# Attention scores on 32-row products of four row groups, in a perceiver kernel on one core

## The chip, the cores and the metric

The kernel runs on one core of one Trainium2 chip, as one program written engine by engine: TensorE (PE, with its weight loads PEld), VectorE (DVE), ScalarE (ACT), GpSimd (POOL) and SyncE (SP), which here only issues DMAs. The engines meet at semaphores. The time is that of the core on the device, in microseconds (us), as the median of several runs.

## What is computed

Two batches of 128 latent tokens of 256 features attend to 2048 context rows each, twice, with other blocks between:

```python
x = x + L0_xattn(norm(x), ctx)   # 16 heads of 128, softmax(q k) v, per batch
x = x + L0_attn(norm(x))         # rotary, cosine similarity, a linear mix
x = x + L0_ffn(norm(x))          # top 2 of 8 experts
x = x + L1_xattn(norm(x), ctx)   # below
x = x + L1_attn(norm(x))         # dilated attention in segments of 64
x = x + L1_ffn(norm(x))          # block floating point, silu(gate) * up
```

The change touches the fourth, whose 16 heads have 16 dimensions, and whose queries see the keys of both batches, 4096 in all:

```python
q = quant((x @ Wq + bq) * scale)            # per query and head, 127 levels a side
k = quant(ctx @ Wk + bk)                    # per key and head
v = quant(ctx @ Wv + bv)                    # per head and dimension, over all keys
a = softmax(q @ k.T)                        # 128 x 4096 for a head of a batch
a = round(a / (max(a) / 255)) * (max(a) / 255)
x = x + (a @ v) @ Wp + bp
```

## The kernel before, in words

**Stages.** Until about 440 us the first cross attention runs, as 32 units (a head of a batch each; `sp_cross`, `pool_cross` and their like for PE, ACT and DVE). On the side POOL quantises the second attention's keys, tile by tile of 128 keys (lines 764 to 782), SP turns each tile by a DMA transposition into `kT` (lines 640 to 644), and the mix, the experts and the queries of batch 0 follow. From about 442 to 660 us the quantised attention runs, again as 32 units of a head of a batch, 16 for each batch. The mix, experts and queries of batch 1 and the output, dilated attention and feed-forward of batch 0 are woven into it as side work, at numbered slots, four to a unit (`Side`, `woven`). A short tail follows.

**A unit of the quantised attention.** The scores of a head are eight products of 512 keys. They are computed twice. The *firsts* (`pe_first`) run 12 products ahead, only for the maxima: DVE reduces each (`dve_first`, line 1892), POOL folds eight maxima into a bias. The *seconds* (`pe_second`) run in pairs, and ACT takes the exponential of each pair, 1024 keys, with that bias (`act_exponentials`, line 1885). SP turns each half of the result, 2048 keys, by a DMA transposition (`sp_attention`, line 1980), and PE multiplies the turned half by the values, 16 products of 16 columns (`attend`, line 1908), two units after the unit itself. PE's order in each quarter of a unit is fixed: two seconds, two firsts, in the first two quarters one half of `attend`, then side work. PE waits for exponentials before seconds (`q_exp`), for maxima before firsts (`q_max`; three PSUM banks take turns), for landings before `attend` (`q_turned`). Each engine takes its program in order, so what stands behind a waiting instruction waits too. In SP's queue the transpositions share the order with loads for later stages (`sp_ahead`).

**Scores.** A key has 16 dimensions in a high and a low fp16 part, 32 rows of `kT` for a head. `kT` holds four heads on its 128 partitions, and a product contracts all 128 rows (`pe_scores`, line 1843) against a query tile in which the rows of the other three heads are zero. That tile, `qT`, is made for each batch by POOL, which clears it (`pool_queries`, line 1833), by DVE, which writes the quantised queries twice for high and low (line 1775), by PE, which transposes four tiles (`pe_queries`, line 1793), and by ACT, which copies 32 rows at a time into place, four times (`act_queries`, line 1812). Batch 0 does that at the end of the first cross attention, batch 1 at slots 55 to 60 of the quantised one. `pe_first` waits for ACT's copies of a batch before the first head that uses each; where a side program shares its PSUM bank with `attend`, PE may also have to wait until the copies are done (`pe_leave`).

Of the kernel before, what the change touches and what calls it, by code (L numbers as in the profile page):

```python
# [19 lines left out]
P = 128  # L20
# [37 lines left out]
QUARTERS = 4  # L58

# [26 lines left out]
    kv k_biased v_biased v_abs k_steps k_rounded k_cut k_turned0 k_turned1 mx_steps mx_round mx_done mx_turned  # L86
    v_scale_pe v_scale_dve v_rounded_dve v_rounded_pool
    mix_pe0 mix_act0 mix_dve0 mix_pool0 ex_pe0 ex_act0 ex_dve0 qu_pe0 qu_act0 qu_dve0
    mix_pe1 mix_act1 mix_dve1 mix_pool1 ex_pe1 ex_act1 ex_dve1 qu_pe1 qu_act1 qu_dve1
# [10 lines left out]
CONSTANTS = steps("zeros ones minus_half ident ident16 ident_fp16 iota iota_f q_zeros0 q_zeros1")  # L100
# [10 lines left out]
QU_PE = steps("xT q qT")  # L111
QU_ACT = steps("xT qT0 qT1 qT2 qT3")
# [28 lines left out]
QU_WOVEN = "norm xT q both qT+copies copies1 copies2+copies3"  # L141
# [4 lines left out]
QU_AT = dict(norm=(29, 1), apply=(29, 3), xT=(30, 1), q=(30, 3), both=(31, 0), qT=(31, 2), copies=(31, 3))  # L146
# [65 lines left out]
class Tiles:  # L212


    def __init__(self, nc, stack):
# [18 lines left out]
        self.qT = upper[:, 0:UNITS * P].rearrange("p (b a r c) -> p b a r c", b=B, r=KG, c=P)  # L234
        self.q_both = upper[:, UNITS * P:(UNITS + KG * B) * P].rearrange("p (b h t d) -> p b h t d", b=B, h=H1, t=2)
# [3 lines left out]
        self.kT = sb("kT", [P, H1 // KG, KT * P], FP16)  # L239
# [78 lines left out]
class ContextTiles:  # L318


    def __init__(self, nc, stack):
# [8 lines left out]
        self.k_tmp = sb("k_tmp", [P, D])  # L330
# [4 lines left out]
        self.k_full = sb("k_full", [P, D])  # L335
        self.k_parts = sb("k_parts", [P, 2, H1, 2, HD1], FP16)
# [274 lines left out]
def sp_cross(sp, m, c, d, g, s, t):  # L611
    for u in range(UNITS + 2):
        if u == 0:
            sp.wait_ge(s["qk_mm"], 2)
            sp_load_early(sp, c, d, s, t, 3)
        elif u == 1:
            sp.wait_ge(s["qk_mm"], 3)
            sp_load_pair(sp, c, s, t, FIRST_PAIR)
        elif u + 2 < SPLIT:
            sp.wait_ge(s["qk_mm"], u + 2)  # L620
            sp_load_early(sp, c, d, s, t, u + 2)
# [30 lines left out]
        if u == H0:  # L652
            sp.wait_ge(s["k_turned0"], 16 * H0)
            sp.wait_ge(s["k_turned1"], 16 * H0)
            sp_load_slice(sp, g, s, t, 0)
            sp_load_slice(sp, g, s, t, 1)
# [81 lines left out]
def pool_cross(pool, m, c, d, g, s, side):  # L738
    full = d.k_full.rearrange("p (h d) -> p h d", h=H1)
    for u in range(UNITS + 3):  # L740
# [26 lines left out]
        for kt in (2 * u, 2 * u + 1) if u < H0 else ():  # L767
            ints = d.k_int[:, kt % 2, :].rearrange("p (h d) -> p h d", h=H1)
            scale = spread(d.k_scale[:, kt % 2, :], 2, HD1)
            hi, lo = (d.k_parts[:, kt % 2, :, n, :] for n in range(2))  # L770
# [772 lines left out]
def pe_mix(pe, m, x, s, b, room, at):  # L1543
# [3 lines left out]
    if b > 0:  # L1547
        pe.wait_ge(s["added"], UNITS)
        pe.wait_ge(s[f"qu_act{b - 1}"], QU_ACT["qT3"])
# [194 lines left out]
def dve_queries(dve, m, s, b, room, at):  # L1744
# [29 lines left out]
    for part in range(2):  # L1774
        dve.tensor_scalar(m.q_both[:, b, :, part, :], heads, ROUND, -ROUND, ALU.add, ALU.add).then_inc(sem, 1)


def pe_queries(pe, m, s, b, room, at):
# [10 lines left out]
    yield at["qT"]  # L1789
    pe.wait_ge(s[f"qu_dve{b}"], QU_DVE["both1"])  # L1790
    q_all = flat(m.q_both[:, b])
    for g in range(H1 // KG):
        ins = pe.transpose(room[2].bitcast(FP16)[:, g * P:(g + 1) * P], q_all[:, g * P:(g + 1) * P],
                           m.ident_fp16[:, :])
    ins.then_inc(sem, 1)
    if room.shared:
        yield from pe_leave(pe, room, at["copies3"], s[f"qu_act{b}"], QU_ACT["qT3"])


def act_queries(act, m, s, b, room, at):  # L1800
# [4 lines left out]
    yield at["copies"]  # L1805
    act.wait_ge(s[f"qu_pe{b}"], QU_PE["qT"])
    act.wait_ge(s["constants"], CONSTANTS[f"q_zeros{b}"])
# [20 lines left out]
def pool_queries(pool, m, s, b, room, at):  # L1828
    yield at["norm"]
    pool_normed(pool, m, s, b, NORM["attend"], room, m.x_res[:, b, :], m.xn[:, b, :])  # L1830
    pool.wait_ge(s["v_rounded_dve"], KT // 4)
    pool.wait_ge(s["v_rounded_pool"], KT // 4)
    pool.memset(m.qT[:, b], 0.0).then_inc(s["constants"], 1)
# [28 lines left out]
def pe_second(pe, m, s, u, q):  # L1862
# [10 lines left out]
    for k in range(CHUNK // BLK):  # L1873
        ins = pe_scores(pe, m, u, m.bank(second_place(u, q) + k), q * CHUNK + k * BLK)
# [21 lines left out]
def pe_attention(pe, m, x, s, side):  # L1896
    def attend(z, half):
# [9 lines left out]
        for j in range(KT // NH):  # L1907
            ins = pe.matmul(m.bank(7)[:, h * HD1:(h + 1) * HD1], x.yT[:, z % 2, half * KT // NH + j, :],  # L1908
                            m.v_int[:, half * KT // NH + j, h * HD1:(h + 1) * HD1], start=half == 0 and j == 0,
                            stop=half == 1 and j == KT // NH - 1)  # L1910
# [61 lines left out]
def sp_attention(sp, m, x, a, s, t):  # L1972
    sp.wait_ge(s["pv"], UNITS)
    for u in range(UNITS - 1):
# [8 lines left out]
        sp_ahead(sp, a, s, t, u)  # L1983

# [39 lines left out]
def dve_output(dve, m, x, s, b, half, room, at):  # L2024
# [11 lines left out]
    if b == 0 and half == 0:  # L2036
# [602 lines left out]
```

## Time and profile before

| what | value |
|---|---|
| median of 3 runs | 688.6 us (687.6 to 690.27) |
| profiled execution, span | 687.7 us |
| time around that span, by the profile | none recorded |
| PE, PEld busy | 651.0 us (95%), 410.1 us (60%) |
| DVE, ACT, POOL busy | 576.4 us (84%), 417.5 us (61%), 389.1 us (57%) |
| chain of waits by engine | PE 67%, DVE 21%, ACT 5%, issue 3%, DMA 2% |
| line 1843, score products, 512 of them | 140.4 us busy, mean 389 ns |

The span is cut into engines' busy shares, and a chain of waits leads from the last instruction back to the start. PE's mean of one instruction includes the overlap with the next: PE is pipelined, and on the chain four score products take 0.86 us. An engine that idles off the chain costs nothing. A whole-span share is an average over stages, so the stretches of the quantised attention are read one by one.

### The profile page before, as it was taken

The page shows a single profiled execution, that of the slowest core. Times are in us where ns is not written, and L with a number is a line of the kernel's source. Part 1 is how long each engine was busy: PE and PEld are TensorE (multiplying, and loading weights), DVE is VectorE, ACT ScalarE, POOL GpSimd, SP SyncE. Part 2 cuts the span into 40 slices and gives each one's busy share as a digit, 9 for nine tenths or more (in the row PEclk, how much of TensorE's full clock was granted, in tenths as well). Part 3 has the DMA queues.
Part 4 walks back from the last instruction along what each step waited for, and adds up shares of the span by engine and source line. Part 5 has one row for each costly group of instructions (what it writes and reads, how often), then busy time and mean ns, then how long its engine had stood idle before and what let it go on. Part 6 is the DMA issues. An engine that isn't in the chain of part 4 may idle for free.

```text
span 687.7 us, 13890 instructions
## 1 busy us (share of the span) xinstructions
PE 651.0 (95%) x5088; PEld 410.1 (60%) x5088; DVE 576.4 (84%) x1029; ACT 417.5 (61%) x697; POOL 389.1 (57%) x500
## 2 busy tenths in 40 slices
PE   8899999999999999999999999999889889988887
PEld 6456766666666676766766666654436444544453
DVE  5998987887897797899989769888877889999655
ACT  5644454444544465565654445549878899899941
POOL 5876666566557736689965516526635543345401
PEclk9999999999999999999999999999989999999999
DMA  9666689765756588988974965639998899999900
GB/s 309 164 147 140 146 184 172 173 140 122 158 122 151 120 196 215 210 173 193 184 168 118 226 144 115 148 81 218 235 186 153 168 149 198 160 185 163 201 14 9
DMA packets 347827, 111.01 MB, mean 161 GB/s; under 512 B 313704, under 2 KB 344432, under 8 KB 347760
## 3 DMA queue, kind: packets, MB, share of 16 engines
q1 hardware_dynamic: 347760, 110.13, 77.1%
q8 instruction: 41, 0.67, 0.4%
q14 instruction: 26, 0.21, 0.1%
HBM read 31.97 MB, written 0.26 MB: 47 GB/s over the span
## 4 chain that ended last, share of the span: by engine, by line
PE 67%; DVE 21%; ACT 5%; issue 3%; DMA 2%; POOL 1%; DVEq 0%; ACTq 0%; POOLq 0%
PE psum L1060 21%; PE psum L1032 20%; DVE tops L1892 8%; PE psum L1843 6%; PE psum L1046 5%; PE psum L506 3%; ACT cT L1885 3%; DVE neg_max L1272 2%; PE psum L1908 2%; DMA c_nat<-cT 2%; PE psum L1085 1%; PE psum L1095 1%; PE psum L827 1%; PE psum L845 1%; DVE e_lo L1260 1%
## 5 line engine op out<-in xcount | busy, mean ns | idle before, releaser
L1060 PE MATMUL psum<-c_nat,eT 128*128 128x256 f16 x1536 | 188.1, 273 | 0.9 <-ACT u_sb L1234 0.9
L1892 DVE TENSOR_REDUCE tops<-psum 128x1 f32<-128x512 f32 x256 | 159.6, 683 | 20.7 <-PE psum L1843 20.1
L1885 ACT ACTIVATE cT<-psum,bias,q_scale 128x1024 f16<-128x1024 f32 x128 | 153.5, 1204 | 22.6 <-PE psum L1843 21.1
L1032 PE MATMUL psum<-cT,qk 128*128 128x512 f16 x744 | 165.6, 379 | 0.1
L1060 PEld LDWEIGHTS psum<-c_nat,eT 128*128 128x128 f16 x1536 | 147.3, 98 | 24.1 <-issue 1.6
L1843 PE MATMUL psum<-kT,v_space 128*128 128x512 f16 x512 | 140.4, 389 | 9.4 <-DVE tops L1892 7.3
L1032 PEld LDWEIGHTS psum<-cT,qk 128*128 128x128 f16 x744 | 72.6, 98 | 82.3 <-issue 1.2
L1272 DVE TENSOR_REDUCE neg_max<-psum 128x1 f32<-128x2048 f32 x32 | 73.2, 2287 | 21.3 <-PE psum L1032 21.2
L1260 DVE TENSOR_TENSOR e_lo<-e_all,e_hi 128x2048 f16<-128x2048 f32 x32 | 88.5, 2767 | 0.0
L1843 PEld LDWEIGHTS psum<-kT,v_space 128*128 128x128 f16 x512 | 45.4, 99 | 71.4 <-DVE tops L1892 34.4
L1203 ACT ACTIVATE e_all<-psum,neg_max 128x2048 f32<-128x2048 f32 x32 | 63.1, 1970 | 16.5 <-DVE neg_max L1274 16.4
L858 ACT ACTIVATE qT<-psum 128x128 f32<-128x128 f32 x31 | 8.6, 279 | 100.8 <-PE psum L827 91.2
L776 POOL TENSOR_TENSOR k_full<-k_int,k_scale 128x256 f32<-128x256 bf16 x32 | 26.7, 836 | 72.1 <-issue 46.9
L1208 ACT CAST e_hi<-e_all 128x2048 f16<-128x2048 f32 x32 | 60.8, 1898 | 1.6 <-DMA eT<-e_hi 0.6
L2012 POOL TENSOR_SCALAR least<-least,tops 128x1 f32<-128x1 f32 x64 | 23.1, 361 | 51.5 <-DVE tops L1892 50.5
L1046 PE MATMUL psum<-wkv,cT 128*128 128x512 f16 x192 | 46.7, 379 | 2.5 <-DVE k_tmp L1326 2.5
L1908 PEld LDWEIGHTS psum<-v_space,c_nat 128*128 128x128 f16 x1024 | 33.9, 96 | 22.4 <-DMA c_nat<-cT 6.4
L746 POOL TENSOR_TENSOR u_parts<-u_sb,u_parts 128x256 f16<-128x256 f32 x30 | 31.7, 1056 | 21.8 <-ACT u_parts L1239 21.7
L1908 PE MATMUL psum<-v_space,c_nat 128*128 128x16 f16 x1024 | 35.4, 170 | 8.3 <-DMA c_nat<-cT 4.0
L777 POOL TENSOR_TENSOR k_parts<-k_int,k_scale 128x256 f16<-128x256 bf16 x32 | 40.9, 1278 | 0.0
L749 POOL TENSOR_TENSOR wvo_parts<-wvo_h,wvo_parts 128x512 f16<-128x512 f32 x30 | 36.7, 1222 | 0.0
L759 POOL TENSOR_TENSOR wqk_parts<-wqk_h,wqk_parts 128x512 f16<-128x512 f32 (+1 forms) x27 | 31.7, 1175 | 0.3
(286 smaller groups left out, 947.3 us busy)
## 6 DMA issues: line engine op xcount, KB each, us to landing
wvo_h<-in_L_xattn_Wv SPq DMA_DIRECT2D x30, 128.0 KB, 2.4
wvo_h<-in_L_xattn_Wo SPq DMA_DIRECT2D x30, 128.0 KB, 2.3
wqk_h<-in_L_xattn_Wq SPq DMA_DIRECT2D x28, 128.0 KB, 2.4
wqk_h<-in_wkT SPq DMA_DIRECT2D x28, 128.0 KB, 2.6
mx_land<-in_mx_weights SPq DMA_DIRECT2D x8, 384.0 KB, 4.0
v_space<-in_ctx SPq DMA_DIRECT2D x4, 512.0 KB, 5.8
cT<-in_ctx SPq DMA_DIRECT2D x2, 1024.0 KB, 8.3
c_nat<-in_expert_wT SPq DMA_DIRECT2D x2, 1024.0 KB, 6.6
```

The source lines that it names most:

```text
L777: pool.tensor_tensor(hi, ints, scale, ALU.mult).then_inc(s["k_cut"], 1)
L1032: ins = pe.matmul(s_ps[:, n * 512:(n + 1) * 512], c.qk[:, u % 2, q_part, k, :], m.cT[:, b, c_part, 4 * n:4 * n + 4, k, :], start=(k, q_par ...
L1046: ins = pe.matmul(kv_ps, m.cT[:, kt // KTB, c_part, kt % KTB, k, :], d.wkv[w_part][:, k, :], start=(k, w_part, c_part) == (0, 0, 0), stop= ...
L1060: ins = pe.matmul(u_ps, c.eT[:, v % 2, e_part, j, :], m.c_nat[:, v // H0, c_part, j, :], start=(j, e_part, c_part) == (0, 0, 0), stop=(j, ...
L1203: act.activation(c.e_all[:, :], s_ps, ACT.Exp, bias=c.neg_max[:, u % 2:u % 2 + 1], scale=1.0 / UP, accum_out=c.row_sum[:, u:u + 1]).then_i ...
L1208: act.copy(c.e_hi[:, :], c.e_all[:, :]).then_inc(s["e_hi"], 1)
L1260: dve.tensor_tensor(c.e_lo[:, :], c.e_all[:, :], c.e_hi[:, :], ALU.subtract).then_inc(s["e_lo"], 1)
L1272: dve.tensor_reduce(limit, s_ps, AX.X, ALU.max, negate=True).then_inc(s["max"], 1)
L1843: return pe.matmul(ps, m.qT[:, b, group, r, :], m.kT[:, group, at:at + BLK], start=True, stop=True)
L1885: act.activation(m.y[:, u % 2, q * CHUNK:(q + 1) * CHUNK], m.bank(second_place(u, q), 2), ACT.Exp, bias=m.bias[:, u:u + 1], scale=m.q_scal ...
L1892: dve.tensor_reduce(m.tops[:, n // NB, n % NB:n % NB + 1], m.bank(n % 3), AX.X, ALU.max, negate=True).then_inc(s["q_max"], 1)
L1908: ins = pe.matmul(m.bank(7)[:, h * HD1:(h + 1) * HD1], x.yT[:, z % 2, half * KT // NH + j, :], m.v_int[:, half * KT // NH + j, h * HD1:(h ...
```

## The change

Keys are cut into four row groups instead of heads: `kT` holds, for every head, 32 rows of 1024 keys on each of four groups of partitions, the four groups being every fourth tile of keys. A score product contracts 32 rows, on the group that its number names (`score_block`), and the firsts take the numbers in another order, so that two seconds and the two firsts behind them lie on four different groups. Keys are turned four tiles at a time. The queries stand four times, once for each group: DVE writes them for group 0, POOL copies them to the other three, SP turns all by one DMA transposition (`sp_queries`), for batch 0 ahead of the last probabilities of the first cross attention, for batch 1 behind unit 12's transpositions. POOL's clearing, PE's transpositions and ACT's copies of the queries go, and two waits of PE and DVE on those copies. `attend` takes the values' tiles in the new order (`key_tile`). The output side work of batch 0 begins four slots earlier, since the queries take fewer slots.

```diff
-        self.kT = sb("kT", [P, H1 // KG, KT * P], FP16)
+        self.kT = sb("kT", [P, H1, KT // KG * P], FP16)
-        self.k_parts = sb("k_parts", [P, 2, H1, 2, HD1], FP16)
+        self.k_parts = sb("k_parts", [P, H1, KG, 2, HD1], FP16)
 def sp_cross(sp, m, c, d, g, s, t):
     for u in range(UNITS + 2):
+        if u == UNITS:
+            sp_queries(sp, m, s, 0)
...
-        if 0 < u <= H0:
-            for kt in (2 * u - 2, 2 * u - 1):
-                sp.wait_ge(s["k_cut"], 3 * kt + 3)
-                sp.dma_start_transpose(m.kT[:, :, kt * P:(kt + 1) * P], flat(d.k_parts[:, kt % 2])).then_inc(
-                    s[f"k_turned{kt % 2}"], 16)
+        if 0 < u <= H0 and u % 2 == 0:
+            n = u // 2 - 1
+            sp.wait_ge(s["k_cut"], 3 * KG * (n + 1))
+            sp.dma_start_transpose(m.kT[:, :, n * P:(n + 1) * P], flat(d.k_parts)).then_inc(s["k_turned"], 16)
...
-            if kt > 1:
-                pool.wait_ge(s[f"k_turned{kt % 2}"], 16 * (kt // 2))
+            if kt > 0 and kt % KG == 0:
+                pool.wait_ge(s["k_turned"], 16 * (kt // KG))
...
     for part in range(2):
-        dve.tensor_scalar(m.q_both[:, b, :, part, :], heads, ROUND, -ROUND, ALU.add, ALU.add).then_inc(sem, 1)
+        dve.tensor_scalar(m.q_rows[:, b, :, 0, part * HD1:(part + 1) * HD1], heads, ROUND, -ROUND, ALU.add,
+                          ALU.add).then_inc(sem, 1)
...
-    yield at["qT"]
-    pe.wait_ge(s[f"qu_dve{b}"], QU_DVE["both1"])
-    q_all = flat(m.q_both[:, b])
-    for g in range(H1 // KG):
-        ins = pe.transpose(room[2].bitcast(FP16)[:, g * P:(g + 1) * P], q_all[:, g * P:(g + 1) * P],
-                           m.ident_fp16[:, :])
-    ins.then_inc(sem, 1)
-    if room.shared:
-        yield from pe_leave(pe, room, at["copies3"], s[f"qu_act{b}"], QU_ACT["qT3"])
...
-    for r in range(KG):
-        if room.shared and r > 0:
-            yield at[f"copies{r}"]
-        rows = slice(r * DW, (r + 1) * DW)
-        act.copy(m.qT[rows, b, :, r, :], room[2].bitcast(FP16)[rows, 0:H1 // KG * P].rearrange(
-            "p (g c) -> p g c", c=P)).then_inc(sem, 1)
...
-    pool.memset(m.qT[:, b], 0.0).then_inc(s["constants"], 1)
+    yield at["spread"]
+    pool.wait_ge(s[f"qu_dve{b}"], QU_DVE["both1"])
+    pool.tensor_copy(m.q_rows[:, b, :, 1:KG, :], spread(m.q_rows[:, b, :, 0, :], 2, KG - 1)).then_inc(
+        s["qu_pool"], 1)
+def sp_queries(sp, m, s, b):
+    sp.wait_ge(s["qu_pool"], b + 1)
+    sp.dma_start_transpose(m.qT[:, b], flat(m.q_rows[:, b])).then_inc(s["qu_turned"], 16)
+def score_block(n):
+    return 2 * (n // 2 % 2) + n % 2, n // KG
+def key_tile(n):
+    group, column = score_block(n // KG)
+    return KG * (KG * column + n % KG) + group
-def pe_scores(pe, m, u, ps, at):
-    b, group, r = u // H1, u % H1 // KG, u % KG
-    return pe.matmul(ps, m.qT[:, b, group, r, :], m.kT[:, group, at:at + BLK], start=True, stop=True)
+def pe_scores(pe, m, u, ps, n):
+    group, column = score_block(n)
+    rows, cols = slice(group * DW, (group + 1) * DW), slice(column * BLK, (column + 1) * BLK)
+    return pe.matmul(ps, m.qT[rows, u // H1, u % H1, :], m.kT[rows, u % H1, cols], start=True, stop=True)
...
-    if n % NB == 0 and n // NB % H1 < KG:
-        pe.wait_ge(s[f"qu_act{n // (NB * H1)}"], QU_ACT[f"qT{n // NB % H1}"])
+    if n % (NB * H1) == 0:
+        pe.wait_ge(s["qu_turned"], 16 * (n // (NB * H1) + 1))
...
-    pe_scores(pe, m, n // NB, m.bank(n % 3), n % NB * BLK).then_inc(s["q_first"], 1)
+    pe_scores(pe, m, n // NB, m.bank(n % 3), n % NB ^ 2).then_inc(s["q_first"], 1)
...
         sp_ahead(sp, a, s, t, u)
+        if u == QU_TURNED:
+            sp_queries(sp, m, s, 1)
...
-    if b == 0 and half == 0:
-        dve.wait_ge(s["qu_act1"], QU_ACT["qT3"])
```

Three lines are added above `pe_scores`, so lines of the quantised attention stand two or three further down in the changed kernel (1843 becomes 1846, 1892 becomes 1895, 1908 becomes 1911, 1980 becomes 1982).

On SP, in the queue of the quantised attention, the names being those of the buffers (`c_nat` the turned, `cT` the unturned probabilities), the end of the list was, and is now:

```order
293 L1453 DMA wp<-in_L_xattn_Wp 128x2x256
294 L1454 DMA bp<-in_L_xattn_bp 128x256
295 L1455 DMA sets<-in_dil_sets 128x200
296 L1980 DMA_TRANSPOSE c_nat<-cT 128x16x128 [waits q_pv,q_exp] x52
297 L2590 DMA out<-x_res 128x256 [waits written] x2
```

```order
286 L1454 DMA wp<-in_L_xattn_Wp 128x2x256
287 L1455 DMA bp<-in_L_xattn_bp 128x256
288 L1456 DMA sets<-in_dil_sets 128x200
289 L1982 DMA_TRANSPOSE c_nat<-cT 128x16x128 [waits q_pv,q_exp] x16
290 L1824 DMA_TRANSPOSE v_space<-v_space 128x16x128 [waits qu_pool]
291 L1982 DMA_TRANSPOSE c_nat<-cT 128x16x128 [waits q_pv,q_exp] x36
292 L2592 DMA out<-x_res 128x256 [waits written] x2
```

One transposition, the queries', has come between the 16 of units 5 to 12 and the 36 of units 13 to 30, and it waits for POOL.

On PE, around the first product for batch 1 (the one that waits for the queries), the rows were, and are now:

```order
876 L1908 MATMUL psum<-v_space,c_nat 128x16 [waits q_turned01]
877 L1908 MATMUL psum<-v_space,c_nat 128x16 x15
878 L1793 MATMUL psum<-ident_fp,v_space 128x128 [waits qu_dve1]
879 L1793 MATMUL psum<-ident_fp,v_space 128x128 x3
880 L1843 MATMUL psum<-kT,v_space 128x512 [waits q_exp]
881 L1843 MATMUL psum<-kT,v_space 128x512
882 L1843 MATMUL psum<-kT,v_space 128x512 [waits q_max,qu_act1]
883 L1843 MATMUL psum<-kT,v_space 128x512 [waits q_max]
```

```order
871 L1911 MATMUL psum<-v_space,c_nat 128x16 [waits q_turned01]
872 L1911 MATMUL psum<-v_space,c_nat 128x16 x15
873 L1846 MATMUL psum<-kT,v_space 128x512 [waits q_exp]
874 L1846 MATMUL psum<-kT,v_space 128x512
875 L1846 MATMUL psum<-kT,v_space 128x512 [waits q_max,qu_turned]
876 L1846 MATMUL psum<-kT,v_space 128x512 [waits q_max]
877 L2077 MATMUL psum<-ident,att 128x128 [waits at_dve0]
878 L1846 MATMUL psum<-kT,v_space 128x512 [waits q_exp]
```

The four transpositions are gone, the first product waits for the landing of the turned queries instead of ACT's copy, and an output product stands behind it.

## Rows read from the trace of the kernel before

**Rows 1.** Page, part 1: busy us (share of span) xinstructions.
```profile
PE 651.0 (95%) x5088; PEld 410.1 (60%) x5088; DVE 576.4 (84%) x1029; ACT 417.5 (61%) x697; POOL 389.1 (57%) x500
```

**Rows 2.** Page, part 4: the chain of waits by line, share of the span.
```profile
PE psum L1060 21%; PE psum L1032 20%; DVE tops L1892 8%; PE psum L1843 6%; PE psum L1046 5%; PE psum L506 3%; ACT cT L1885 3%; DVE neg_max L1272 2%; PE psum L1908 2%; DMA c_nat<-cT 2%; PE psum L1085 1%; PE psum L1095 1%; PE psum L827 1%; PE psum L845 1%; DVE e_lo L1260 1%
```

**Rows 3.** Windows: us; PE, PEld, DVE, ACT, POOL busy; granted clock; DMA share.
```profile
463.00:508.00 45.00, 38.87 (x327) 18.81 (x326) 35.80 (x62) 38.02 (x67) 25.45 (x57) 0.94 1.11 216
508.00:548.00 40.00, 37.92 (x337) 21.78 (x335) 33.20 (x67) 35.27 (x62) 21.04 (x44) 0.98 0.90 165
548.00:562.00 14.00, 11.55 (x103) 5.56 (x104) 11.56 (x24) 12.01 (x21) 5.32 (x14) 0.88 0.80 136
562.00:649.00 87.00, 78.72 (x783) 39.40 (x782) 83.51 (x161) 79.32 (x142) 39.84 (x99) 1.00 1.05 183
```

**Rows 4.** Waits, 463 to 508: waiter, awaited, us, times, longest.
```profile
PEld psum L1908 <- DMA c_nat<-cT: 6.4, 5, 2.9
```

**Rows 5.** Chain of waits, 548 to 557: start, us, what.
```profile
548.39 0.47 DVE v_space L1775 x2
...
550.89 0.25 PE psum L1793 x4
...
551.17 0.58 ACT v_space L1812
...
554.88 0.58 ACT v_space L1812
...
555.48 0.59 ACT v_space L1812
...
556.11 0.56 PE psum L1908 x16
```

**Rows 6.** Groups, 562 to 649: count, busy us, mean ns, idle before, releasers.
```profile
L1892 DVE TENSOR_REDUCE tops<-psum 128x1 f32<-128x512 f32 x117 | 72.5, 683 | 0.6 <-PE psum L1843 0.3
```

**Rows 7.** Groups, 463 to 649 us, DVE's reductions and ACT's exponentials.
```profile
L1892 DVE TENSOR_REDUCE tops<-psum 128x1 f32<-128x512 f32 x236 | 146.8, 683 | 17.4 <-PE psum L1843 17.0
L1885 ACT ACTIVATE cT<-psum,bias,q_scale 128x1024 f16<-128x1024 f32 x120 | 143.9, 1203 | 17.5 <-PE psum L1843 16.0 <-issue 0.5 <-DMA c_nat<-cT 0.2
```

**Rows 8.** Chain of waits around 520 to 523 us.
```profile
520.73 0.86 PE psum L506 x4
521.59 0.86 PE psum L1843 x4
522.45 0.38 PE psum L1908 x16
```

**Rows 9.** Timeline of PE around 537 us: start us, us, engine, line, operation.
```profile
537.43 0.69 PE L1712 MATMUL psum<-v_abs,coefT 8*128 8x256 f32 x2
```

**Rows 10.** Line 776 on POOL (keys): what ended its idle time, us, times.
```profile
  issue: 46.9, 11
```

**Rows 11.** Line 1980 (y transpositions) with landing; POOL's cast, line 730.
```profile
L1980 SPq DMA_TRANSPOSE c_nat<-cT x62: 1657/2137/3813, 457.0 to 649.5; - x62
...
DMA to landing us min/median/max: 4.3/4.6/7.1
...
L730 POOL CAST c_nat<-v_space x2: 1030/1033/1036, 5.9 to 9.1; 128x1024 f16<-128x1024 f32 x2
```

**Rows 12.** Timeline of PE around 435 us; chain of waits around 442 us.
```profile
435.32 0.40 PE L1793 MATMUL psum<-ident_fp,v_space 128*128 128x128 f16 x4 [0.76 <-DVE v_space L1775]
...
442.44 0.43 PE psum L1843 x2
```

**Rows 13.** Chain of waits, 497 to 509; windows of 2 us.
```profile
497.21 6.14 DMA c_nat<-cT
...
504.00 5.13 PE psum L1843 x12
...
501.00:503.00 2.00, 0.00 (x0) 0.00 (x0) 1.08 (x2) 0.87 (x2) 1.39 (x3) 0.94 1.28 79
503.00:505.00 2.00, 1.60 (x19) 0.86 (x20) 0.00 (x0) 0.10 (x1) 0.22 (x1) 0.50 1.17 263
```

More of the change, by code:

```diff
@@ L58 @@
 QUARTERS = 4
+QU_TURNED = 12
 BLK = 512
@@ L110 @@
 EX_DVE = steps("logits best gap where where_f plus_one first second coef0 coef1 coef a0 a1 a2 a3 a4 a5 a6 a7 bias")
-QU_PE = steps("xT q qT")
-QU_ACT = steps("xT qT0 qT1 qT2 qT3")
+QU_PE = steps("xT q")
+QU_ACT = steps("xT")
 QU_DVE = steps("biased amax clamp inverse over up both0 both1")
@@ L140 @@
     "prod7+add6 coefT+add7 bias add8"
-QU_WOVEN = "norm xT q both qT+copies copies1 copies2+copies3"
+QU_WOVEN = "norm xT q both+spread"
 OUT_WOVEN = ("gather0 yT0 out0 added0", "gather1 yT1 out1 added1")
@@ L145 @@
     "units1 scaled1 round1 back1 pause mT1 down"
-QU_AT = dict(norm=(29, 1), apply=(29, 3), xT=(30, 1), q=(30, 3), both=(31, 0), qT=(31, 2), copies=(31, 3))
+QU_AT = dict(norm=(29, 1), apply=(29, 3), xT=(30, 1), q=(30, 3), both=(31, 0), spread=(31, 0))
 def spread(ap, dim, n):
@@ L318, with __init__ @@
 class ContextTiles:
-    def __init__(self, nc, stack):
+    def __init__(self, nc, stack, m):
         def sb(name, shape, dt=F32):
@@ L329, in __init__ @@
         self.bkv = sb("bkv", [P, 2 * D])
-        self.k_tmp = sb("k_tmp", [P, D])
+        self.k_tmp = m.xn[:, 0, :]
         self.k_amax = sb("k_amax", [P, H1])
@@ L652, in sp_cross @@
         if u == H0:
-            sp.wait_ge(s["k_turned0"], 16 * H0)
-            sp.wait_ge(s["k_turned1"], 16 * H0)
+            sp.wait_ge(s["k_turned"], 16 * KT // KG)
             sp_load_slice(sp, g, s, t, 0)
@@ L769, in pool_cross @@
             scale = spread(d.k_scale[:, kt % 2, :], 2, HD1)
-            hi, lo = (d.k_parts[:, kt % 2, :, n, :] for n in range(2))
+            hi, lo = (d.k_parts[:, :, kt % KG, n, :] for n in range(2))
             pool.wait_ge(s["k_rounded"], kt + 1)
-            if kt > 1:
-                pool.wait_ge(s[f"k_turned{kt % 2}"], 16 * (kt // 2))
+            if kt > 0 and kt % KG == 0:
+                pool.wait_ge(s["k_turned"], 16 * (kt // KG))
             if kt > 0:
@@ L1548, in pe_mix @@
         pe.wait_ge(s["added"], UNITS)
-        pe.wait_ge(s[f"qu_act{b - 1}"], QU_ACT["qT3"])
+        pe.wait_ge(s["qu_turned"], 16 * b)
     pe.wait_ge(s["mix_in"], 16 * 7)
@@ L1873, in pe_second @@
     for k in range(CHUNK // BLK):
-        ins = pe_scores(pe, m, u, m.bank(second_place(u, q) + k), q * CHUNK + k * BLK)
+        ins = pe_scores(pe, m, u, m.bank(second_place(u, q) + k), q * CHUNK // BLK + k)
     ins.then_inc(s["q_second"], 1)
@@ L1906, in attend @@
             pe.wait_ge(s["at_dve0"], AT_DVE["over_sum1" if z > H1 else "over_sum0"])
[L1907 to L1910, printed above, removed]
+        for j in range(half * KT // NH, (half + 1) * KT // NH):
+            ins = pe.matmul(m.bank(7)[:, h * HD1:(h + 1) * HD1], x.yT[:, z % 2, j, :],
+                            m.v_int[:, key_tile(j), h * HD1:(h + 1) * HD1], start=j == 0, stop=j == KT - 1)
         ins.then_inc(s["q_pv"], 1)
@@ L2523, in perceiver @@
             with ExitStack() as half:
-                d = ContextTiles(nc, half)
+                d = ContextTiles(nc, half, m)
             with ExitStack() as half:
@@ L2553, in perceiver @@
             queries = woven(QU_WOVEN, experts["add8"] + 1)
-            output = woven(OUT_WOVEN[0], queries["copies3"] + 1) | woven(OUT_WOVEN[1], NC * (H1 + 1) + 1)
+            output = woven(OUT_WOVEN[0], queries["both"] + 1) | woven(OUT_WOVEN[1], NC * (H1 + 1) + 1)
             dilated = woven(DIL_WOVEN, output["added1"] + 1)
```

17 lines of the change are left out of this document (6 added, 11 removed).

## The prediction

> **What bounds the kernel now.** I read the page first: busy times, then the chain of waits by line. TensorE (PE) is busy 651.0 of 687.7 us [rows 1], which looks as if any shortening of it were a gain. The chain says otherwise: the score products of line 1843, which this change shortens, hold 6% of the span on it, 43 us, while lines 1060 and 1032, which it does not touch, hold 41% [rows 2]. So I went on to the windows, the stage of the scores cut into four stretches [rows 3], and asked in each which resource is full. The reader is to see four different answers.
> - 463 to 508 us: the mean DMA share is 1.11, PE is busy 38.87 of 45. PE's weight load for line 1908, the product with the probabilities, waits 6.4 us in five pieces for transpositions to land [rows 4]. DMA bounds.
> - 508 to 548: PE 37.92 of 40, DMA 0.90, DVE 33.20, ACT 35.27. PE bounds.
> - 548 to 562: queries of batch 1, with ACT's copies on the chain [rows 5].
> - 562 to 649: DVE 83.51 and ACT 79.32 of 87, DMA 1.05. DVE's reductions there wait 0.6 us in all before 117 instructions [rows 6]. DVE bounds, with DMA hardly behind.
>
> Over 463 to 649 the group view gives the most that a faster score product could return: the reductions (tops) stood 17.0 us and the exponentials 16.0 us for line 1843 [rows 7]. These are the same stretches seen from two engines, not 33 us, and part of them is PE itself waiting for DMA.
>
> **What a score block costs, before and after.** Four products of 512 columns take 0.86 us [rows 8], 0.216 each. After the change they contract 32 rows each, and four stand on four row groups. No row of before shows products overlapping on different row groups, so I bound it: none overlap, 0.86; all four do, 0.22. I take 0.22, because the four products of a block have four different groups and no result of one is an operand of another; the other end is a rival. New is also the switch between 128-row and 32-row products. The nearest row is line 1712, two f32 products that contract 8 rows: they take 0.69 us, where two f32 products of line 506 with the same 256 columns take half of 0.86 [rows 8, 9]. That leaves 0.26 us for going in and out; I take 0.25, and as bounds 0 and 0.5. A full block then falls from 0.86 to 0.47, and a block of two products, as they stand where firsts run alone between other work, goes from 0.43 to 0.47.
> The Trainium skill (TensorEngine Tiling (Array Packing), Tiling Modes, Key Properties) says that changing the tiling mode drains the engine: a rule against this change, which switches twice in every quarter of a unit. By line 1712 the rule holds here at 0.26 us per pair of switches, already in the sum; without it a block would cost 0.22 and the sum change by little, since PE then ends ahead of ACT in either case.
>
> **The parts of the change.**
> *Keys, 40 to 240 us: 0.* Eight DMA transpositions of four tiles take the place of 32 of one, and one buffer of four tiles that of two. POOL must now wait at every fourth tile until the buffer has been read. What hides it: POOL stood 46.9 us idle before line 776 with nothing to wait for in that phase [rows 10], and the wait is a landing (4.6 us for y transpositions [rows 11]) before seven of the eight fours, some 32 us. Without that cover each would delay the last key tile by up to 4.6 us. PE, on the chain there, does not read the turned keys until 442 us.
>
> *Queries of batch 0, 434 to 463: -0.8.* PE no longer waits 0.76 us for DVE and no longer transposes 0.40 us [rows 12]: -1.16. In their place DVE's rows are spread by POOL (1536 fp16 elements a partition; 1024 of a cast take 1.033 us [rows 11], so an estimate of 1.55) and turned by one DMA transposition ahead of that of the last probabilities. DVE ends at about 435.3, so they land at 435.3 + 1.55 + 0.1 + 4.6 = 441.5; the first score ran at 442.44 [rows 12] and could now run at 441.3. I count +0.2 for that, and +0.2 for five blocks of two products at 0.04. At 7.1, the longest landing [rows 11], the whole term would be +1.8.
>
> *Scores, 463 to 503: 0.* DMA bounds; a faster PE only waits earlier.
>
> *503 to 508: -1.6.* PE idled until a transposition of 6.14 us landed, and afterwards ran at a granted clock of 0.50 (1.2 GHz), so that twelve score products took 5.13 us [rows 13]. Three blocks on four groups would take 3 x (0.43 + 0.5) = 2.8 us at that level, 2.3 less; but half of the twelve feed three exponentials of 1.20 us [rows 7], 3.6 us, so ACT is late next and 5.13 falls to about 3.5. Bounds: 0 and 2.3.
>
> *508 to 548: -2.3.* Some 24 full blocks give PE 24 x 0.39 = 9.4 us of room. Where it is wholly PE's (the middle of the stretch, expert products between the blocks), a unit is four score blocks of 0.86, three expert blocks of 0.86 and two half heads of 0.38, 6.8 us. ACT was busy 88% of this stretch [rows 3], 6.0 of 6.8 us. So three such units return at most 0.8 each; I take 0.6, 1.8 together, since DMA is 0.90 full, and 0.5 for the other three, where DVE at 0.83 has side work too. ACT is late next, then DMA. Bounds: 0 (ACT and DMA bind at once) and 40 - 35.27 = 4.7.
>
> *Queries of batch 1, 548 to 575: +1.5.* Gone from the chain are PE's four transpositions (0.25) and three copies of ACT (0.58, 0.58, 0.59) [rows 5], 2.0 us, and 0.2 of waits beside them. POOL loses two memsets, which lie beside other work. But the first product of batch 1 now waits for DVE, POOL's spread and a transposition: DVE ends at 548.86 [rows 5], + 1.55 + 0.1 + 4.4 = 554.9, and PE would reach that product at about 551.2: 3.7 us in which it stands, with the seconds, the attends and the output's products queued behind it. SP is the other queue: the order places this transposition between those of unit 12 and unit 13, so SP stands until about 550.5, and both halves of unit 13 are issued behind it, at 2.1 us of SP each [rows 11], about 552.6 and 554.7. They land near 557 and 559; the product that reads the first started at 556.11 [rows 5]. Bounds: -2.2 (the wait is hidden) and +5 (both halves late as well, DMA at 1.05 after it).
>
> *562 to 649: -0.4.* DVE is at 96%; only its 0.6 us of waits can go.
>
> Sum: -0.8 - 1.6 - 2.3 + 1.5 - 0.4 = -3.6. The profiled execution's span is 687.7, the median of the runs 688.6, 0.9 above; so 684.1 as a span, **685.0 us** as a median.
>
> **The rivals.**
> *PE was the bound, and all of its relief comes through.* Then 508 to 548 gives 4.7 and the second batch's queries 2.2, with the other terms as they are: -0.8 - 1.6 - 4.7 - 2.2 - 0.4 = -9.7, about 679. For: 95% PE; against: DMA over 1 in two of four stretches. Chance 0.2. The Trainium skill (TensorE: Matmul & The Clock Gate, Part 3) gives 3.07 times for four row-tiled products of 512 columns: on the chain's 43 us of line 1843 that rule alone would return about 29 us, an estimate of some 659, to which I give 0.02 of the 0.2; the chain before 463 and the reductions that take over after it speak against it.
>
> *Slower: the clock.* Where PE idled from 501 to 503 the grant fell to 0.50 [rows 13]. Faster scores leave PE idle more often: from 508 to 649, 24 units with four blocks each, 96 x 0.39 = 37 us of PE's time would become idle time in pieces. If the grant falls for good in the stretches with little side work, f32 expert products (0.86 to 1.72) and attends double. Price: twelve expert blocks at +0.86 and ten half heads at +0.4 come to 14 us, of which the slack before DVE and ACT (40 - 35.27 [rows 3]) hides a third: +9, less the 3.6, so about 694. It decides from the point where PE stands as long as at 501. Chance 0.2.
>
> *The row groups do not overlap.* Then each full block costs 0.86 + 0.25: 24 in the PE-bound stretch, +6, of which some 2 are hidden, +1.5 for the queries, -0.8 at the start: about 693. Chance 0.15.
>
> **How the numbers follow.** The forecast has 0.45, with 681.5 to 688.5 as its own range. A measurement can tell about 0.5% from no change, 3.4 us. Faster than that, below 685.2: half the forecast (0.24) and the first rival (0.2), 0.44. Slower, above 692.0: most of the clock's case (0.15), of the row groups' (0.10) and 0.03 of the forecast's tail, 0.28. The rest, 0.28, is within. The range leaves out half of the first rival and half of the clock's case: 678.5 to 694.5.
>
> **What would show it.** Right: score blocks near 0.47 us on the chain, PE's busy time between 463 and 649 down by 25 us or more while the stage shortens by 2 to 4; SP standing between unit 12 and 13 until about 550.5 and PE waiting at the first product of batch 1 for the turned queries, near 555; after 562 the same DVE share. Wrong: blocks of 0.86 or more (no overlap); granted clock 0.5 in stretches other than 503 to 509 (the clock); a stage from 463 to 508 that shortens, which would say that DMA did not bound it.

## The result, and the profile after

The changed kernel takes 699.93 us (median of 4 runs, 698.61 to 701.74) where the kernel before took 688.51 beside it: a ratio of 1.0173, 95% interval 1.0155 to 1.0192. It is slower by 11.4 us, outside the predicted range, and on the other side of the forecast. The profiled execution spans 699.0 us, 11.3 more than before.

The page of the changed kernel, parts 1 and 2, shows first that PE is busy longer over the whole span, not shorter ([rows 1]), and then, in the tenths of the granted clock by slices, where: in the last third of the span.

```profile
PE 659.5 (94%) x5080; PEld 400.2 (57%) x5080; DVE 573.9 (82%) x1029; ACT 413.6 (59%) x689; POOL 389.1 (56%) x500
PEclk9999999999999999999999999976568555555589
```

The windows of the changed kernel by the same stretches (columns as in [rows 3]):

```profile
434.00:463.00 29.00, 25.14 (x199) 16.99 (x196) 26.22 (x51) 13.67 (x23) 13.16 (x18) 1.00 0.59 120
463.00:508.00 45.00, 40.34 (x360) 17.72 (x360) 36.91 (x63) 38.47 (x70) 26.38 (x58) 0.58 1.11 219
508.00:548.00 40.00, 35.84 (x320) 17.81 (x318) 33.24 (x70) 34.63 (x62) 19.42 (x42) 0.75 0.82 148
548.00:562.00 14.00, 9.14 (x79) 3.50 (x79) 9.24 (x18) 7.84 (x15) 5.55 (x14) 0.52 1.01 176
562.00:649.00 87.00, 79.76 (x721) 32.67 (x718) 78.27 (x148) 73.36 (x130) 34.82 (x88) 0.50 1.00 171
```

The granted clock falls to 0.50, the lower of its two levels (1.2 GHz), at 463 us, where the units of the quantised attention follow one another. It is back at 1.00 from 480 to 487, from 518 to 535 (expert products stand between the score blocks there) and from 545 to 548, and then 0.50 until 668. But for the wait at 550, PE is at work for nine tenths of the time from 463 to 649; its busy time there is 165.1 us for 167.1 before. In the last stretch DVE does 78.27 us of work in 87 where it did 83.51, ACT 73.36 for 79.32. The group view of 562 to 649 says for whom they wait:

```profile
L1895 DVE TENSOR_REDUCE tops<-psum 128x1 f32<-128x512 f32 x109 | 68.4, 681 | 3.4 <-PE psum L1846 2.8
L1888 ACT ACTIVATE cT<-psum,bias,q_scale 128x1024 f16<-128x1024 f32 x56 | 67.1, 1204 | 12.6 <-PE psum L1846 11.9 <-DMA c_nat<-cT 0.5
```

DVE's wait before its reductions was 0.6 us [rows 6] and is 3.4, with 109 of them done for 117. PE has become the bound of a stretch in which it had not been one. The chains of waits from 575 to 600 us say the same, of the change and then of run 4 below, in which the clock is as low but the score products are short: the score products (L1846, L1847) hold 28.7% of the change's stretch and DVE's reductions (tops) 10.0%, in run 4 5.0% and 23.3%.

```profile
by line: PE psum L1846 28.7%; PE psum L1911 11.1%; DVE tops L1895 10.0%; PE psum L2183 9.1%; PE psum L2187 6.9%; ACT cT L1888 5.0%; PE psum L2178 4.6%; PE psum L2170 3.8%; DVE top L2158 3.5%; DVE sc L2160 3.5%; DVE apart L2129 3.1%; PE psum
by line: DVE tops L1896 23.3%; PE psum L2184 9.1%; ACT cT L1889 7.3%; PE psum L2188 6.9%; PE psum L2202 6.2%; PE psum L1912 5.7%; PE psum L1847 5.0%; issue 4.8%; PE psum L2179 3.9%; PE psum L2171 3.8%; DVE sc L2161 3.5%; DVE top L2159 3.5%;
```

The row groups do overlap where four products stand ready together. The chain of waits, at half clock (508) and at full (521 and 534), against 0.86 for a block of four [rows 8]. Where they do not, as around 577 and 580 at half clock, five in a row hold the chain for 2.33 us and four for 1.45:

```profile
508.55 0.55 PE psum L1846 x4
...
521.37 0.41 PE psum L1846 x4
...
533.74 0.33 PE psum L1846 x4
534.07 0.49 PE psum L1911 x16
...
577.47 2.33 PE psum L1846 x5
579.80 0.53 PE psum L1911 x16
580.32 1.45 PE psum L1846 x4
```

And the wait for batch 1's queries came as described. The chain around 548, then SP's timeline:

```profile
546.86 1.47 POOL v_space L1817
548.34 0.02 issue
548.35 5.44 DMA v_space<-v_space
553.79 0.05 issue
553.84 0.60 PE psum L1846 x2
```

```profile
535.53 4.80 SPq L1982 DMA_TRANSPOSE c_nat<-cT  x2
548.35 1.76 SPq L1824 DMA_TRANSPOSE v_space<-v_space  x1
550.20 17.30 SPq L1982 DMA_TRANSPOSE c_nat<-cT  x6
```

Where the 11.3 us came from can be read from the start of each unit's first exponential. The change is 0.7 us ahead at unit 0, 1.4 behind at unit 7 and 2.8 ahead at unit 8, since unit 7 takes 4.82 us where it took 9.00 with the late transposition of [rows 13]. It is still 2.8 ahead at unit 13. It gives all of that back in units 13 to 15 (7.47, 12.16 and 4.74 us for 6.46, 8.54 and 6.20) and is 0.35 behind at unit 16. Units 16 to 31 take 101.5 us for 92.3, and the tail, which begins at half clock, 1.7 more.

Within the same kernel, units at full clock gain. Units 10 and 11 lie in the stretch from 518 to 535, at 0.99, and take 6.38 and 6.00 us for 6.93 and 6.50. There PE is busy for less of the time, while DVE and ACT get more done (first before, then after, columns as in [rows 3]):

```profile
518.00:535.00 17.00, 16.73 (x135) 10.50 (x132) 12.76 (x21) 15.78 (x27) 8.82 (x19) 1.00 0.86 152
518.00:535.00 17.00, 14.98 (x173) 8.76 (x172) 13.86 (x23) 16.43 (x31) 9.10 (x21) 0.99 0.85 148
```

### The profile page after: what moved, and what is told of

It reads as the page before. It is cut to its first block and busy times, and to the rows that moved or that the text cites. A ratio compares the mean times of both kernels' runs of the same rounds, so it can differ in the third digit from the quotient of the medians.

```text
span 699.0 us, 13832 instructions
## 1 busy us (share of the span) xinstructions
PE 659.5 (94%) x5080; PEld 400.2 (57%) x5080; DVE 573.9 (82%) x1029; ACT 413.6 (59%) x689; POOL 389.1 (56%) x500
## 5 line engine op out<-in xcount | busy, mean ns | idle before, releaser
L1846 PE MATMUL psum<-kT,v_space 32*128 32x512 f16 x512 | 111.6, 556 | 14.3 <-DVE tops L1895 5.9
L1846 PEld LDWEIGHTS psum<-kT,v_space 32*128 32x128 f16 x512 | 24.0, 97 | 77.6 <-DVE tops L1895 31.7
L777 POOL TENSOR_TENSOR xn<-k_int,k_scale 128x256 f32<-128x256 bf16 x32 | 23.7, 740 | 70.7 <-DVE k_int L1341 38.6
L1911 PEld LDWEIGHTS psum<-v_space,c_nat 128*128 128x128 f16 x1024 | 32.2, 103 | 28.9 <-issue 17.2
L778 POOL TENSOR_TENSOR k_parts<-k_int,k_scale 128x256 f16<-128x256 bf16 x32 | 46.9, 1464 | 0.0
L747 POOL TENSOR_TENSOR u_parts<-u_sb,u_parts 128x256 f16<-128x256 f32 x30 | 31.5, 1050 | 23.4 <-ACT u_parts L1240 23.3
L1911 PE MATMUL psum<-v_space,c_nat 128*128 128x16 f16 x1024 | 37.7, 174 | 3.6 <-DVE mid L2306 1.0
L2014 POOL TENSOR_SCALAR least<-tops 128x1 f32<-128x1 f32 x32 | 12.1, 379 | 43.1 <-DVE tops L1895 42.9
```

Source lines behind the costliest of these rows:

```text
L778: pool.tensor_tensor(hi, ints, scale, ALU.mult).then_inc(s["k_cut"], 1)
L1846: return pe.matmul(ps, m.qT[rows, u // H1, u % H1, :], m.kT[rows, u % H1, cols], start=True, stop=True)
```

## The experiments

The theory after that result: the 32-row products take the clock away, and the query path costs some microseconds more. Rivals: the clock fell because PE stood more often; the loss is the query path, and the clock a bystander.

**1. 128 rows with everything else of the change.**

```diff
-    rows, cols = slice(group * DW, (group + 1) * DW), slice(column * BLK, (column + 1) * BLK)
+    rows, cols = slice(0, P), slice(column * BLK, (column + 1) * BLK)
```

> The changed kernel with one edit: each score product contracts all 128 rows of its columns instead of the 32 rows of its group (the scores are then sums over four key tiles, another computation of the same shape). Keys, queries, DMAs and order are those of the change. If the fall of the granted clock is the cause of the loss, the clock is back at 0.97 or more, the units 16 to 30 take 5.8 us each as before, and the time is 689 to 693, the query path of batch 1 (some 3 us in unit 14) being what is left. If the loss lay in the query path or in the key layout, the time stays at 697 or more.

Measured: 692.12 us, ratio 1.0067 (1.0047 to 1.0087), mean granted clock 0.993, that of the kernel before. The windows:

```profile
463.00:508.00 45.00, 38.36 (x328) 18.67 (x326) 35.34 (x61) 37.58 (x66) 25.14 (x56) 0.96 1.08 213
508.00:548.00 40.00, 37.91 (x348) 21.87 (x347) 34.05 (x70) 36.08 (x64) 20.26 (x45) 1.00 0.88 156
548.00:562.00 14.00, 9.00 (x87) 4.59 (x84) 8.85 (x18) 7.10 (x13) 5.58 (x12) 0.76 0.87 152
562.00:649.00 87.00, 78.79 (x777) 38.74 (x775) 84.81 (x161) 79.49 (x143) 39.51 (x99) 1.00 1.10 186
```

So 7.8 of the 11.4 us hang on the rows, and some 4 on the rest. Units 16 to 31 take 92.5 us, as before; units 10 and 11 take 6.93 and 6.50, as before; unit 14 takes 12.71.

**2. 32 rows, all on one group.** PE is now at work as long as 128 rows would keep it, or longer.

```diff
+    rows, cols = slice(0, DW), slice(column * BLK, (column + 1) * BLK)
```

> The changed kernel with every score product on rows 0 to 31 (four key tiles of the heads are left out, one is used four times): still 32 rows and the same switches, but no two products can overlap, so PE is as long at work as before. If the clock fell because PE idles more, it stays at 0.97 or more and the time is 690 to 695. If the clock fell because 32-row products count for little, however long PE is at work on them, it falls as in the changed kernel or further (0.87 or less), and the time is 700 to 720, a block taking 0.9 us at full clock and 1.75 at half.

Measured: 804.66 us, ratio 1.169, clock 0.807. The windows of this run:

```profile
463.00:508.00 45.00, 45.00 (x220) 17.37 (x220) 25.32 (x42) 27.50 (x48) 17.68 (x38) 0.50 0.78 157
508.00:548.00 40.00, 40.00 (x212) 15.70 (x210) 23.20 (x47) 22.42 (x37) 12.25 (x31) 0.50 0.62 121
```

The clock fell at 462 us, PE having been at work for 1.54 of the 2 us before, and was back at 773. From 463 to 508 PE was at work for 45.00 of 45.00 us, and the grant stayed at 0.50. So standing is not needed for the lower level: with 128 rows in the same order (run 1) PE was at work for 38.36 of the same 45 us and was granted 0.96. The clock came out as the second expectation has it, the time 85 us above its range, which had not reckoned with half clock throughout. The chain of this run gives the switch as well: a block takes 1.81 us, where a 128-row block at this clock would take 2 x 0.86 = 1.72 us, an estimate from [rows 8]; the switch is then 0.09.

```profile
504.63 0.53 PE psum L1911 x16
505.16 1.81 PE psum L1846 x4
```

**3. 64 rows, on one half.**

```diff
+    rows, cols = slice(0, P // 2), slice(column * BLK, (column + 1) * BLK)
```

> The changed kernel with every score product on rows 0 to 63 (two key tiles summed, the others left out): no two can overlap, so PE is at work as long as with 128 rows or with 32 rows of one group. If the grant goes by the rows in use, the clock lies between the two, 0.85 to 0.97, and the time between 700 and 790. If any tile smaller than the whole array counted alike, it is that of one group, 0.81 and 804.

Measured: 803.22 us, clock 0.811, as with 32. The expected level between was not seen. In both runs the clock was at its lower level nearly all through the stage, so they can show no difference between 32 and 64 rows:

```profile
508.00:548.00 40.00, 40.00 (x212) 15.93 (x211) 23.19 (x47) 22.41 (x37) 12.18 (x31) 0.50 0.62 120
```

**4. All rows, a quarter of the columns.** The products have 128 rows again, but from unit 2 on three quarters of the keys are left out.

```diff
+    width = BLK if u < 2 else 128
+    rows, cols, ps = slice(0, P), slice(column * BLK, column * BLK + width), ps[:, 0:width]
```

> Score products of 128 rows with a quarter of the columns (128 of 512; from unit 2 on three quarters of the keys are left out, and DVE and ACT read old sums for them): a block takes PE 0.22 us, a little less than the change's 0.33, and works the whole array for as long as four overlapping 32-row products do. If the grant goes by the work of the array, rows times time, the clock falls as in the changed kernel, 0.85 to 0.90, and the time is 692 to 700. If small tiles are what counts for little, the clock stays at 0.97 or more and the time is 683 to 690.

Measured: 692.51 us, clock 0.881 (the change: 0.873).

**5. Half the columns.** The edit is the same with 256.

> The same with half the columns (256 of 512), 0.43 us a block. If the grant goes by the work of the array, the clock lies between those of the quarter and of the whole, 0.89 to 0.97, and the time is 690 to 698. If small tiles alone count for little, 0.97 or more and 685 to 691.

Measured: 689.27 us, ratio 1.0011 (0.9996 to 1.0026), clock 0.948, as the first expectation has it; the time is 0.7 below its range. The windows of 562 to 649 of the quarter, then of the half:

```profile
562.00:649.00 87.00, 64.83 (x764) 43.55 (x761) 81.61 (x157) 77.75 (x137) 38.11 (x96) 0.52 1.08 183
```

```profile
562.00:649.00 87.00, 70.20 (x775) 43.53 (x773) 80.46 (x156) 78.09 (x137) 38.15 (x95) 0.77 1.07 184
```

Whole, half, quarter: 1.00, 0.77, 0.52 in this stretch, and 0.50 in the change. With fewer columns PE also stands more (64.83 of 87 us at work with a quarter), so runs 4 and 5 by themselves do not tell whether the time at work or the columns took the clock; run 2 shows a fall that the time at work does not explain. Both ways tried of shortening the scores on PE lower the clock here.

What the quarter says of the time: at nearly the same clock the change is 7.4 us slower. Units 16 to 31 take 95.3 us in run 4, 92.5 in run 1 and 101.5 in the change. So half clock with short score products costs some 2.7 us there, and the other 6.3 hang on the 32-row products at that clock. Two costs in their rows are there for it, but were not taken apart: the switch, 0.09 for a block and about 0.07 for a half head at this clock (0.52 for 0.45, start to start), and that a first that waits for DVE starts alone, while a product that does not overlap takes its full time (0.45 in the block of run 2, 1.81 for four).

**6. More work for PE, to hold the clock.** Ahead of each pair of seconds, one or two 128-row products of 512 columns into the banks that the pair then overwrites.

```diff
+    for k in range(1):   # 2 in the second run
+        pe.matmul(m.bank(second_place(u, q) + k), m.qT[:, u // H1, u % H1, :], m.kT[:, u % H1, 0:BLK], start=True,
+                  stop=True)
```

> The changed kernel with one product of 128 rows and 512 columns ahead of each pair of seconds, written to the pair's first bank and overwritten by it: 0.22 us more work for PE in each block, 128 products in all. If the clock is the cause, more work makes it faster: clock 0.93 or more, time 688 to 695. If PE's work is the cause, it is slower than the changed kernel by some 5 to 15 us.

> The same with two such products ahead of each pair, one for each bank: 0.43 us more in each block, 256 products. If the clock is the cause: clock 0.97 or more, time 686 to 692, what is left being the query path of batch 1. If PE's work is the cause, slower than the changed kernel by 10 to 30 us.

Measured: one, 710.7 us and clock 0.892; two, 700.97 and 0.993. With one the time is what the rival said, 10.8 us over the change: the clock rises from 0.873 to 0.892 only, and much of the added work is paid at half clock. Two miss both expectations: they hold the clock, but the time is the change's. Against run 1, at the same clock, they cost 9 us. The chain of the run with two, at full clock:

```profile
641.95 0.60 PE psum L1877 x2
642.55 0.41 PE psum L1846 x4
642.96 0.49 PE psum L1914 x16
643.45 0.45 PE psum L1877 x2
643.90 0.33 PE psum L1846 x4
```

Filler, block and half head take 0.45 + 0.33 + 0.49 = 1.27 at best, where a 128-row block and a half head take 0.86 + 0.38 [rows 8]: nothing is saved, and the filler stands ahead of the pair for which ACT waits. So no run brings the clock back and keeps the gain of the overlap.

**7. The query path.** At half clock and at full clock, batch 1's queries turned behind unit 13.

```diff
-QU_TURNED = 12
+QU_TURNED = 13
```

> The changed kernel with the turning of batch 1's queries placed behind unit 13's transpositions instead of unit 12's, so that SP no longer holds unit 13 back while it waits for POOL. The queries land when they did, near 554. If the clock carries the loss, only unit 14 to 16 can gain: 0 to 2 us, 698 to 700, clock still 0.88. If SP's standing were the main loss: 692 or less.

> The run with 128 rows of a column in each score product (another computation of the same shape), with the queries' turning behind unit 13. At full clock that run was 4.0 us slower than the kernel before, and its unit 14 took 12.7 us for 8.5. If SP's standing makes half of it or more: 688 to 690. If PE's wait for the landing alone makes it: 691 to 692.5.

Measured: 699.91 us in the change, no difference; 691.46 with 128 rows, 0.7 less than run 1, which their intervals (1.0028 to 1.0074 here) do not tell apart. By its expectation that speaks for the landing.

**8. No wait for the landing.** Batch 1's scores read batch 0's turned queries, at 128 rows.

```diff
-    if n % (NB * H1) == 0:
-        pe.wait_ge(s["qu_turned"], 16 * (n // (NB * H1) + 1))
+    if n == 0:
+        pe.wait_ge(s["qu_turned"], 16)
...
-    return pe.matmul(ps, m.qT[rows, u // H1, u % H1, :], m.kT[rows, u % H1, cols], start=True, stop=True)
+    return pe.matmul(ps, m.qT[rows, 0, u % H1, :], m.kT[rows, u % H1, cols], start=True, stop=True)
```

> The run with 128 rows in each score product, in which batch 1's scores take batch 0's turned queries (another computation) and wait for no landing; POOL's spread and SP's transposition for batch 1 are still made, behind unit 12. If PE's wait for the landing is what is left of the loss, the time falls by 3 to 5 us, to 687 to 689. If SP's standing and the late unit 13 are: by less than 1.5 us.

Measured: 693.15, no gain, which by its expectation speaks for SP's standing, against run 7. PE's timeline says why each edit alone gives nothing: with the wait gone PE stands for the halves of unit 13 that SP held back (first view); with those in time (run 7 at 128 rows, second view) it stands for the queries.

```profile
557.22 0.55 PE L1911 MATMUL psum<-v_space,c_nat 128*128 128x16 f16 x16 [2.76 <-DMA c_nat<-cT]
557.62 1.02 PE L1846 MATMUL psum<-kT,v_space 128*128 128x512 f16 x4
560.73 0.60 PE L1911 MATMUL psum<-v_space,c_nat 128*128 128x16 f16 x16 [2.08 <-DMA c_nat<-cT]
```

```profile
555.32 1.04 PE L1846 MATMUL psum<-kT,v_space 128*128 128x512 f16 x2 [4.57 <-DMA v_space<-v_space]
```

**9. Both edits.** The diffs of runs 7 and 8 together, at 128 rows.

> Products of 128 rows, batch 1's queries turned behind unit 13, and batch 1's scores from batch 0's turned queries without a wait (another computation): both edits that by themselves gave 0.7 us and nothing. If the two waits stand in parallel (PE for the queries' landing, or PE for the late halves of unit 13, whichever is left), both must go: the time falls by 4 us or more against the run with 128 rows alone, to 685 to 688. If something else in the query path or the earlier output slots makes the loss, it stays at 690 or more.

Measured: 686.45 us, ratio 0.9967 (0.9953 to 0.9981): 5.7 less than run 1. Unit 14 takes 7.28 us, where it took 12.71 in run 1 and 13.18 and 10.35 in runs 7 (128 rows) and 8; in run 8 the rest moved to unit 15. Two waits stood side by side, and either is enough.

**10. The mend in whole computations.** Queries spread and turned in two parts, heads 0 to 3 first, behind unit 13: in the change, and in the change with two fillers in every unit but 0 and 9 to 12.

```diff
+    for n, (heads, sem) in enumerate(((slice(0, KG), "qu_turned"), (slice(KG, H1), "k_turned"))):
+        sp.wait_ge(s["qu_pool"], 2 * b + n + 1)
+        sp.dma_start_transpose(m.qT[:, b, heads], flat(m.q_rows[:, b, heads])).then_inc(s[sem], 16)
...
+    for k in range(0 if u == 0 or 9 <= u <= 12 else 2):
```

> The changed kernel, whole computation, with batch 1's queries spread and turned in two parts, heads 0 to 3 first, behind unit 13's transpositions: the mend of both waits in unit 14. At 128 rows the two waits together were worth 5.7 us. If they are worth as much at half clock: 694 to 697. If PE at half clock only moves its lateness to the units behind: 698 or more.

> The changed kernel, whole computation, with two full products ahead of each pair of seconds in every unit but 0 and 9 to 12 (those have f32 expert products between their blocks), the queries of batch 1 spread and turned in two parts, heads 0 to 3 first, and turned behind unit 13. If the clock holds (0.97 or more), units 9 to 12 gain some 2 us on the kernel before, unit 14 loses its waits, and the others lose 0.1 to 0.3 each to the switches: 688 to 694, which would be level with the kernel before at best. If the full products are needed in units 9 to 12 too, the clock is 0.93 to 0.97 and the time 694 to 700.

Measured: the change so mended 697.46 us, ratio 1.0132 (1.0103 to 1.0162), clock 0.872; PE's wait for the queries is 1.50 us for the change's 4.4 (a wait of the change, then PE's timeline of this run), and 2.5 us come through. With fillers 693.93, ratio 1.0065 (1.0045 to 1.0086), clock 0.983: the best of the kernels with 32-row products, and still slower than before.

```profile
PE psum L1846 <- DMA v_space<-v_space: 4.4, 1, 4.4
```

```profile
552.74 0.60 PE L1848 MATMUL psum<-kT,v_space 32*128 32x512 f16 x2 [1.50 <-DMA v_space<-v_space]
```

**11. The query path without the row groups.** The kernel before, with its 128-row products and keys; DVE writes the queries into rows that POOL has cleared, and SP turns them in two parts.

```diff
+    for r in range(KG):
+        dve.tensor_scalar(m.q_rows[:, b, :, r, r], spread(heads.rearrange("p (a r) d -> p a r d", r=KG)[:, :, r], 2, 2),
+                          ROUND, -ROUND, ALU.add, ALU.add).then_inc(sem, 1)
```

> The kernel before with its 128-row products, key layout and zero-padded query tiles, whole computation; only the queries are made as rows with zeros by DVE (four writes of 128 elements in place of two of 256) and turned by DMA in two parts, heads 0 to 3 first, for batch 1 behind unit 13; no PE transpositions, no ACT copies, no spread by POOL. The clock stays at 0.99. If the waits are mended by that, the gain is that of the run without a wait, less some 1 us for the first landing: 686 to 688, 0.1 to 0.4% faster than before. If the landings of the queries hold PE as in the change: 689 to 692.

Measured in 12 runs: 687.52 us, ratio 0.9982 (0.9966 to 0.9999), clock 0.993. PE waits 1.15 us where the change waited 4.4:

```profile
551.32 1.03 PE L1838 MATMUL psum<-kT,v_space 128*128 128x512 f16 x2 [1.15 <-DMA v_space<-v_space]
```

It is the one whole computation here that is ahead of both kernels, by about 1 us, which is hardly more than the runs can tell.

## Why the prediction was wrong, point by point

**The full block: right, and better than said.** It was put at 0.47 us with a switch of 0.25; on the chain at full clock it takes 0.33 where all four overlap and 0.41 where one is a little late, and the switch shows in two places, at least 0.11 in the block (0.33 less 0.22) and 0.10 in the half head behind it (0.49 for 0.39). The rival without overlap is out. But the sum took every block for a full one, and where firsts wait for DVE the four do not stand ready together.

**The start, put at -0.8: not shown.** Unit 0 begins 0.7 us earlier than before in the one profile (452.13 for 452.84). In run 7, the same program up to unit 12, it begins at 452.84. The agreement is within what two profiles differ by. Of the key phase nothing shows.

**463 to 503, put at 0, and 503 to 548, put at -3.9: half of it came, and from unit 7 alone.** Units 0 to 6 lost 2.1 us, at a clock of 0.50 for much of the time. Unit 7 gained 4.2, for which 1.6 had been put: the transposition that was late in [rows 13] was not waited for. What of that the row groups gave is not shown: run 9, with 128 rows and up to unit 12 the same program as run 1, took 12.9 us for units 6 and 7, where run 1 took 15.5 and the change 12.4. Units 8 to 12, put at -2.3, gave 0.0: units 10 and 11, at full clock, gained 0.55 and 0.50, near the 0.6 that was put, and units 8 and 9, mostly at half clock, lost 0.6 and 0.7.

**The queries of batch 1, put at +1.5: right in mechanism, and near in size.** Units 14 and 15 take 2.2 us more than before, unit 13 another 1.0. The queries landed at 553.8 where 554.9 was said; SP stood until 548.3, and the halves of unit 13 were late as described. The two waits that the upper bound of +5 adds up stand side by side, as runs 7 to 9 show; the mend must treat both.

**562 to 649, put at -0.4: wrong, and this is the step that failed.** Units 16 to 31 measured +9.2 us. "DVE is at 96%; only its 0.6 us of waits can go" counted DVE's bound as fixed, and with it the clock at which PE serves DVE. At 0.50 PE came late and DVE fell to 78.27 of 87 us. What ran at 1.2 GHz was the rest of PE's work (f32 products of the side work, half heads) and the score products themselves, which overlapped only in part there. By runs 1 and 4 half clock with short score products costs some 2.7 us of the 9.2; the other 6.3 hang on the 32-row products at that clock, and how much of it is the switch and how much the missing overlap stays open.

**PE's busy time, said to fall by 25 us or more between 463 and 649.** It fell by 2.0, at 0.50 for most of that time. The sign that the prediction gave for the clock's case, 0.5 in stretches other than 503 to 509, is what came.

**The rival of the clock named the event and missed its condition.** It put the point at "PE stands as long as at 501", with a chance of 0.2 and a price that led to 694. Its price for half heads, 0.4 each, is not what came: start to start they take 0.45 at half clock in run 4 and 0.40 at full clock in run 1. Run 2 shows the lower level with PE at work without a gap. The evidence read before was a fall behind an idle PE [rows 13], and that reading took a sufficient case for the condition; no row of before has 32-row products beside a granted clock. The Trainium skill (TensorE: Matmul & The Clock Gate, Part 1) says that activity releases the throttle and warns of idle gaps. Run 2, at 0.50 with 45.00 of 45.00 us at work, shows the lower level without such a gap. The Trainium skill (TensorE: Matmul & The Clock Gate, Part 3) gives 3.07 times for four row-tiled products of 512 columns. The trace is somewhat below it for a full block with its switch, 2.1 to 2.6 times (0.86 to 0.41 or 0.33), and shows a cost on the rest of PE's work beside it.

## What to carry to other kernels

Before PE's work is packed, ask what else PE does in that stage, and what the stage would take at half clock: here a stage that was not bound by PE became so when its products were made smaller and the grant fell. Read the granted clock next to PE's busy share: PE can be busy because it runs at 0.50. Ask also whether the products that are to overlap stand ready together. And where two waits end near each other, take both away in one run before either is called harmless.

## What the runs showed of the hardware that was not expected

- PE at work for 45.00 of 45.00 us (463 to 508) was granted 0.50 with products of 32 rows on one group; with 128 rows (run 1) it was granted 0.96 over the same stretch. With 64 rows it was at work for 40.00 of 40.00 us (508 to 548) at 0.50.
- Four 32-row products of 512 columns on four row groups took 0.33 to 0.41 us at full clock and 0.55 at half. On one row group four took 1.81 at half (run 2).
- Sixteen products of 128 by 16 took 0.45 us at half clock (run 4) and 0.40 at full (run 1), start to start, far from twice as long.
- With 128 rows and a whole, a half and a quarter of the columns, the mean granted clock of the span was 0.993, 0.948 and 0.881.
- Leaving out half of the scores' columns took run 1's time from 692.12 to 689.27 us; leaving out three quarters brought it back to 692.51.
- A transposition of 128 by 2048 fp16 landed in 5.44 us on a queue that had stood since 540, longer than the median of 4.6 [rows 11].
